# Routing by chunks with ScalarE normalising, and experts that gather their rows: one change to a two-layer graph and expert kernel on one core

## What is computed

```python
x = x + L0_gnn(layernorm(x), ...)
x = x + L0_ffn(layernorm(x))      # top 2 of 8 experts
x = x + L1_gnn(layernorm(x), ...)
x = x + L1_ffn(layernorm(x))      # top 1 of 8, with a capacity
# L0_ffn, on xt = layernorm(x):
probs = softmax(xt @ Wr + br)
top_p, top_idx = top_k(probs, 2); weights = top_p / top_p.sum(-1)
xn = layernorm(xt)                # normalised once more
xe = xn * ln_g[e] + ln_b[e]
y = gelu(xe @ W1[e] + b1[e]) @ W2[e] + b2[e]
out = sum of weights * y over the two experts chosen
# L1_ffn, on x = layernorm(x), C = ceil(1.25 * 6250 / 8):
idx = argmax(probs); pos = place of the token in its expert's list
y = (relu(x @ w1[e] + b1[e]) @ w2[e] + b2[e]) * probs[idx] * (pos < C)
y = nan_to_num(y, nan=0.0, posinf=10000.0, neginf=-10000.0)
```

## Time and profile before

| | us |
|---|---|
| median of 3 runs | 6620.97 (6618.58 to 6625.28) |
| profiled run | 6623.49 |
| its span in the trace | 6621.3 |
| plan, node and edge phases of layer 0 | 0 to 2479.2 |
| routing, layer 0 | 2479.2 to 2832.4 |
| experts, layer 0 | 2832.4 to 3662.2 |
| node and edge phases of layer 1 | 3662.2 to 5902.3 |
| routing, layer 1 | 5902.3 to 6163.3 |
| experts, layer 1 | 6163.3 to 6621.3 |

### The profile page before, as it was taken

The page is one execution under the profiler, slowest core; times in us unless marked ns, Lnnn a source line. Parts: engine busy times, 40 slices in busy tenths (PEclk is TensorE's granted clock), DMA queues, the critical chain, the costliest instruction groups (busy, mean ns, idle before and its releaser), DMA issues. The chain is left out here.

```text
span 6621.3 us, 95822 instructions
## 1 busy us (share of the span) xinstructions
PE 4812.8 (73%) x19729; PEld 3525.1 (53%) x19729; DVE 3271.2 (49%) x5938; ACT 1384.0 (21%) x2978; POOL 3635.1 (55%) x3707
## 2 busy tenths in 40 slices
PE   0699999999999982189999435655656565643798
PEld 0355555555555552179999424444444344433698
DVE  5666676666667657211111334444444453544244
ACT  1333333333333320022222201111111111101122
POOL 1677777777777730512222177777777777711322
PEclk9899999999999995589999768888888888875899
DMA  7565565655656626256666555555555555532455
GB/s 214 181 169 159 158 162 157 161 161 157 162 159 160 161 72 216 73 169 184 183 183 184 134 139 137 143 137 142 138 141 139 140 141 138 141 110 109 169 200 188
DMA packets 717638, 1021.21 MB, mean 154 GB/s; under 512 B 301763, under 2 KB 531271, under 8 KB 692316
## 3 DMA queue, kind: packets, MB, share of 16 engines
q0 software_dynamic: 183456, 485.95, 28.4%
q1 hardware_dynamic: 488760, 491.67, 24.8%
q10 hardware_dynamic: 45188, 41.42, 2.1%
HBM read 868.25 MB, written 152.93 MB: 154 GB/s over the span
## 5 line engine op out<-in xcount | busy, mean ns | idle before, releaser
L760 POOL DMA_INDIRECT e_rows<-sc_table,e_eidx x3224 | 3138.4, 973 | 1049.4 <-issue 956.3
L867 PE MATMUL e_ps_o<-e_rows,e_oh 128*128 128x264 f32 x6448 | 1655.6, 401 | 150.1 <-ACT e_res L953 134.3
L867 PEld LDWEIGHTS e_ps_o<-e_rows,e_oh 128*128 128x128 f32 x6448 | 1214.2, 196 | 588.5 <-issue 415.4
L1126 DVE TENSOR_TENSOR e_rows<-e_rows,e_ps_w 128x1024 f32<-128x1024 f32 x806 | 969.8, 1206 | 25.4 <-ACT e_rows L949 14.0
L1058 DVE SCALAR_TENSOR_TENSOR e_u<-e_encr,e_adst,e_ps_hd 128x512 f32<-128x512 f32 x806 | 593.2, 744 | 516.6 <-PE e_ps_X L809 414.0
L809 PE MATMUL e_ps_X<-e_u,e_hwide 128*104 128x512 f32 x1612 | 806.0, 593 | 0.0
L953 ACT COPY e_res<-e_ps_o 32x264 f32<-32x264 f32 x806 | 296.7, 368 | 2122.1 <-PE e_ps_o L871 1710.2
L1670 PE MATMUL x_ps_h<-x_xT,x_w 128*128 128x256 f32 x2624 | 647.8, 405 | 14.1 <-DMA x_b<-in_L_ffn_b_dram 14.1
L1670 PEld LDWEIGHTS x_ps_h<-x_xT,x_w 128*128 128x128 f32 x2624 | 638.3, 337 | 19.0 <-issue 14.9
L839 PE MATMUL e_ps_X<-e_ident,e_alog 128*104 128x128 f32 x496 | 100.3, 367 | 747.7 <-ACT e_alog L933 747.7
L1681 PE MATMUL x_ps_y<-x_w,x_hT 128*128 128x256 f32 x2624 | 579.9, 379 | 0.0
(11 more groups left out here) (290 smaller groups left out, 4067.1 us busy)
## 6 DMA issues: line engine op xcount, KB each, us to landing
x_w<-in_L_ffn_W_dram SPq DMA_DIRECT2D x112, 1024.0 KB
e_at<-sc_grp SPq DMA_DIRECT2D x403, 192.0 KB
x_w<-in_L_ffn_w_dram SPq DMA_DIRECT2D x60, 1024.0 KB
e_rows<-sc_table,e_eidx POOLq DMA_INDIRECT x3224
e_at<-sc_grp SPq DMA_DIRECT2D x403, 96.0 KB
sc_agg<-e_res ACTq DMA_DIRECT2D x806, 33.0 KB
sc_xb<-r_zero SPq DMA_DIRECT2D x24, 1032.0 KB
x_xin<-sc_xb SPq DMA_DIRECT2D x86, 258.0 KB
```

The costliest lines, as they stand in the source:

```text
L760: pool.indirect_dma_start(rows[:, k, s, j, :], None, dr["table"][:, :], bass.IndirectOffsetOnAxis(eidx[:, k, s, j:j + 1], 0)).then_inc(s_r ...
L867: nc.tensor.matmul(ps_o[:, 0:ROW], oh[:, k, at_j:at_j + P], rows[:, k, s, j, :], start=(j == 0), stop=False)
L1126: nc.vector.tensor_tensor(part, part, ps_w[:, k, :, s * HEADS:(s + 1) * HEADS].unsqueeze(3).to_broadcast([P, CH, HEADS, DH]), ALU.mult).th ...
```

## The change

**Routing.** The statistics are now finished chunk by chunk: `combine(c)` adds and takes statistics of chunk c, `finish(c-1)` turns the deviation that ACT made of the chunk before into a scale and an offset. ACT normalises each tile with these (L1411) and copies the turned tiles of two tiles before. PE turns `r_xt` directly, in three PSUM slots, and multiplies. In layer 0 the second normalising is folded into the scale, and the logits are multiplied by `r_std` in turn. SP saves the normalised rows once in token order, `xn0` (258 floats a row) or `xn1` (514, with the token's own row behind it), with each token's weights as 8 bytes behind its row. `xb`, its zeros and POOL's 98 and 49 scatters are gone. Slots become lists of tokens on PE: for each tile and choice DVE makes two matrices of zeros and ones, `r_ohl` [128 x 128] (place in a list) and `r_ohh` [128 x n_hi] (which list, times the token's number; n_hi is 120 in layer 0, 72 in layer 1), and PE sums `r_ohl`^T `r_ohh` over all tiles in `r_ps_t`: 98 products in layer 0, 49 in layer 1, through a ring of 14.

**Experts.** POOL gathers the rows of a block, two transfers a block, by `x_take`, a copy of a piece of the list. It gathers blocks 0 and 1 ahead of the loop; in the loop, for block n, it waits for s_add of block n, gathers block n+2, and then scatters block n. PE's `turn` waits for the gather (s_gx) where it waited for SP's load. SP loads weights only, w1 first. In layer 1 the token's row comes with the gather, so the separate gather of `x_xr` is gone. DVE no longer makes row numbers.

```diff
@@ routing, SP
-                for r0 in range(0, n_slot, 8 * P):
-                    n = min(8, (n_slot - r0) // P)
-                    sp.dma_start(xb[r0:r0 + n * P, :].rearrange("(p j) d -> p (j d)", p=P), zero[:, 0:n * XW]).then_inc(s_fill, 16)
+                    if c >= 2:
+                        keep_rows(c - 2)
+                    if c >= 4:
+                        even_rows(c - 4)
...
+                sp.wait_ge(s_wq, 1)
+                with nc.allow_non_contiguous_dma(reason="a token's weights behind its row, once"):
+                    sp.dma_start(xn[0:NP, D:XW].rearrange("(t p) d -> p t d", p=P), wgt[:, :, :]).then_inc(s_rows, 16)
@@ routing, POOL
-                for t in range(NT):
-                    pool.indirect_dma_start(xb[:, :], bass.IndirectOffsetOnAxis(slot_i[:, 0, t:t + 1], 0),
-                                            xt[:, t, :], None).then_inc(s_top[t // R], 16)
...
@@ routing, PE
+                for t in range(NT):
+                    turn(t)
+                    if t >= 2:
+                        logits(t - 2)
...
+                for n in range(top * NT):
+                    pe.wait_ge(s_ohl, n + 1)
+                    pe.wait_ge(s_ohh, n + 1)
+                    nc.tensor.matmul(ps_t[:, 0:n_hi], ohl[:, n % (2 * R), :], ohh[:, n % (2 * R), :],
+                                     start=(n == 0), stop=(n == top * NT - 1)).then_inc(s_inv, 1)
@@ routing, ACT
+                def even(c):
+                    act.wait_ge(s_nb, c + 1)
+                    for t in range(c * R, (c + 1) * R):
+                        nc.scalar.activation(xt[:, t, :], xs[:, t, :], ACT.Identity, bias=nb[:, t:t + 1], scale=rstd[:, t:t + 1]).then_inc(s_xtn, 1)
+                        if t >= 2:
+                            copy(t - 2)
...
@@ routing, DVE
+                for c in range(R):
+                    combine(c)
+                    if c >= 1:
+                        finish(c - 1)
+                finish(R - 1)
...
+                    for t in range(NT):
+                        n = c * NT + t
+                        if n >= 2 * R:
+                            v.wait_ge(s_inv, n - 2 * R + 1)
+                        nc.vector.tensor_scalar(ohh[:, n % (2 * R), :], iotah[:, :], hi[:, c, t:t + 1], mark[:, c, t:t + 1],
+                                                ALU.is_equal, ALU.mult).then_inc(s_ohh, 1)
+                        nc.vector.tensor_scalar(ohl[:, n % (2 * R), :], iotap[:, :], lo[:, c, t:t + 1], None, ALU.is_equal).then_inc(s_ohl, 1)
@@ experts, POOL
+                def gather(k):
+                    for s in range(SUB):
+                        pool.indirect_dma_start(xin[:, k, s, :], None, xn[:, :],
+                                                bass.IndirectOffsetOnAxis(take[:, k, s:s + 1], 0)).then_inc(s_gx[k], 16)
...
-                        hold(pool, s_ix, i * 8 + (4 * k + 4), s_pq)
-                        if not first:
-                            for s in range(SUB):
-                                pool.indirect_dma_start(xr[:, k, s, :], None, rows_in[:, :],
-                                                        bass.IndirectOffsetOnAxis(idx[:, k, s:s + 1], 0)).then_inc(s_gx[k], 16)
+                        hold(pool, s_ix, i * 2 + (k + 3), s_pq)
                         hold(pool, s_add, i * 2 + (k + 1), s_pq)
+                        gather(k)
+                        hold(pool, s_give, i * 2 + (k + 1), s_pq)
@@ experts, PE
-                        hold(pe, s_ldx[1 - k], (i + k) * n_ldx + n_ldx, s_pp)
+                        hold(pe, s_gx[1 - k], (i + k) * n_sc + n_sc, s_pp)
+                        if first:
+                            hold(pe, s_ldx[1 - k], (i + k) * n_ldx + n_ldx, s_pp)
                         turn(1 - k)
```

More of the change, by code:

```diff
@@ L1226, in ffn_phases @@
         cnt_i = keep("cnt_i", [1, 4], I32)
+        token = keep("token", [P, n_hi], I32)
+        choice = keep("choice", [P, n_hi, 2], F32)
         with ExitStack() as ctx:
@@ L1266, in ffn_phases @@
             ps_c = ps("ps_c", [P, 2, 512])
+            ps_t = ps("ps_t", [P, 512])
             s_x = [sem(f"x{c}") for c in range(R)]
             s_ag = [sem(f"ag{c}") for c in range(2)]
[L1269 to L1277, removed]
+            s_w, s_const, s_zero, s_chain, s_stat, s_var, s_std, s_nb, s_agu, s_xtn = (
+                sem(n) for n in ("w", "const", "zero", "chain", "stat", "var", "std", "nb", "agu", "xtn"))
+            s_t, s_xT, s_l, s_pick, s_cnt, s_soft, s_exp, s_wq, s_slot, s_ohl, s_ohh, s_inv, s_kept, s_rows = (
+                sem(n) for n in ("t", "xT", "l", "pick", "cnt", "soft", "exp", "wq", "slot", "ohl", "ohh", "inv", "kept", "rows"))
             block = ctx.enter_context(nc.Block())
@@ L1364, in logits @@
                     mm.then_inc(s_l, 1)
[L1366 to L1372, removed]
+                for t in range(NT):
+                    turn(t)
+                    if t >= 2:
+                        logits(t - 2)
+                logits(NT - 2)
+                logits(NT - 1)
@@ L1430, in _ @@
                         nc.vector.bn_stats(st[:, t, :], xs[:, t, :]).then_inc(s_stat, 1)
[L1432 to L1435, removed]
+                    v.wait_ge(s_stat, (c + 1) * R)
+                    m, d = mean[:, tiles], dif[:, :]
+                    tt(m, st[:, tiles, 1], st[:, tiles, 4], ALU.add)
                     ts(m, m, 0.5, None, ALU.mult)
-                    tt(d, st[:, :, 1], st[:, :, 4], ALU.subtract)
+                    tt(d, st[:, tiles, 1], st[:, tiles, 4], ALU.subtract)
@@ L1476, in red @@
                     done(nc.vector.tensor_reduce(o, i, AX_X, op))
+                ts(valid[:, :], iotan[:, :], float(N), None, ALU.is_lt)
+                v.wait_ge(s_l, NT)
+                if first:
+                    tt(lg[:, :, :], ps_l[:, 0:NT, :], wide(std[:, 1, :]), ALU.mult)
+                    tt(lg[:, :, :], lg[:, :, :], each(br[:, :]), ALU.add)
+                else:
+                    tt(lg[:, :, :], ps_l[:, 0:NT, :], each(br[:, :]), ALU.add)
                 red(c1[:, 0, :], lg[:, :, :], ALU.max)
@@ L1586, in ffn_phases @@
             s_gx = [sem(f"gx{k}") for k in range(2)]
-            s_ix, s_add, s_mul, s_fl, s_pq, s_free = (sem(n) for n in ("ix", "add", "mul", "fl", "pq", "free"))
+            s_ix, s_give, s_wc, s_wt, s_add, s_mul, s_fl, s_pq, s_free = (
+                sem(n) for n in ("ix", "give", "wc", "wt", "add", "mul", "fl", "pq", "free"))
             n_sc = 16 * SUB
-            n_ldx = 16 * (3 if first else 1)
+            n_ldx = 16 * 2
             n_ldw = 16 * 4
@@ L1646, in _ @@
                         pool.sem_inc(s_free, 1)
+                for k in range(2):
+                    hold(pool, s_gx[k], pairs * n_sc + n_sc, s_pq)
             @block.tensor
@@ L1728, in _ @@
                         affine(1 - k)
+                        hold(v, s_gx[k], i * n_sc + n_sc, s_pv)
+                        nc.vector.tensor_copy(take[:, k, :], token[:, bass.ds((i * 2 + (k + 2)) * SUB, SUB)]).then_inc(s_ix, 1)
+                        if first:
+                            nc.vector.tensor_tensor(wc[:, k, :, :], xin[:, k, :, D:XW], choice[:, bass.ds((i * 2 + k) * SUB, SUB), :],
+                                                    ALU.mult).then_inc(s_wc, 1)
+                            hold(v, s_wc, i * 2 + (k + 1), s_pv)
+                            nc.vector.tensor_reduce(wt[:, k, :], wc[:, k, :, :], AX_X, ALU.add).then_inc(s_wt, 1)
+                        hold(v, s_free, i * 2 + (k + 1), s_pv)
+                        nc.vector.tensor_copy(give[:, k, :], token[:, bass.ds((i * 2 + k) * SUB, SUB)]).then_inc(s_give, 1)
                         hold(v, s_y, i * 2 + (k + 1), s_pv)
-                        hold(v, s_free, i * 2 + (k + 1), s_pv)
                         for s in range(SUB):
```

283 lines of the change are left out of this document (151 added, 132 removed).

## The result

The changed kernel takes 6852.05 us in the median (6843.97 to 6857.54, 4 runs); the kernel before took 6620.36 beside it. The ratio is 1.0349 (95% interval 1.0336 to 1.0362): 3.5% slower. The forecast was slower, with 6645 and a range up to 6740; the direction held and the size did not, 207 us lie between. The profiled run took 6843.97, with a span of 6842.2.

The account below looks back on a forecast made before the run. It took DVE, then POOL's scatters, to bound layer 0's routing, and PE its experts. Routing -156 and -101, expert loops +104 and +127, clock +45, loop end +5 summed to +24: 6645 us, range 6520 to 6740.

Parts of the forecast that it names:

- A chunk: Routing, layer 0: a chunk of the statistics on DVE takes 12.2 us, where it took 10.51.
- A pair: Routing: two one-hot matrices on DVE and their product on PE, 0.46 us a pair, bounds 0.43 to 0.67.
- The 14 tiles behind the last chunk: Routing, layer 0: 14 tiles left for PE after the last chunk, 14 x 1.18 = 16.5 us, before the logits.
- Layer 1: Expert loop, layer 1: gather lands at 12.2 us, needed at 7.68; +4.7 a block, +127; low clock +45.
- Layer 0, landing: Expert loop, layer 0: gather waits behind weights, lands 9.5 us after h starts, 2.0 late a block: +104, ends 0 and 159.
- Layer 0, clock: Expert loop, layer 0: pauses of 2.0 us cost nothing through a lower PE clock (0 to 85).
- the second rival: Both expert loops: the clock falls after each pause, adding 53 x 1.6 us in layer 0: 6730; chance 0.12.
- The first rival: Expert loop, layer 0: gather lands before 7.68 us, so the 104 falls away: 6541, faster; chance 0.30.
- hidden parts: Routing, layer 0: row saving and 6272 weight pieces stay covered by other work; if not, 5 to 10 us.
- the loop's end: End of the expert loops: the last scatters stand behind two more gathers, 2 x 2.6 = +5 us.

Follow-up runs that it names:

- weights behind the issue: Changed kernel, but in layer 0 SP waits with a block's weights until POOL has issued both gathers: 6746.7 us.
- w1 in four: Changed kernel, but in layer 0 w1 is loaded as four transfers of 256 KB instead of one of 1 MB: 6739.5 us.

## Why the prediction was right in direction and wrong in size

**Routing: right in its sums, one step by luck.** -157 and -99 against -156 and -101. A chunk takes 11.9 (said 12.2); logits came 118.4 after the routing's start (said 116.1). A pair costs 0.45 to 0.46 (said 0.46), but on DVE (0.255 + 0.195): the forecast took its number from a row of PE and had DVE's pair between 0.33 and 0.48, so the match is luck. That PE's clock rose there to 0.84 and more (0.59 is the stage's mean) changed nothing, since DVE sets the pitch. The 14 tiles behind the last chunk were seen; that ACT's order, too, holds them was not.

**Layer 1: right.** The chain on DVE, POOL's issue and the landing made 12.66 us against 12.35 (12.2 and 0.15 from landing to turning), the gathers issued 0.6 sooner than said and the rest 0.9 longer; 4.8 of pause a block against 4.7; and the clock cost about 2.3 a block against 1.6.

**Layer 0, landing: the step that failed.** The sum took the landing at 9.5 us after the h phase's start; its upper end, 159 us, stands for 10.5. It was 11.7. The wait behind w1 was not the error: a landing at 9.5 has the first packet 2.2 before it, at 7.3, and it came at 7.1. What was mis-sized is the time behind that. The 2.3 us that a gather pair takes alone were kept for the time behind w1, and being served among w2's packets was counted as a gain (8 to 9). But there the gathers share the engines with w2 and the first scatter: in the block shown it took 4.0 us from their first packet to the end of their last, where it took 2.0 with no weights, and turning began 0.8 us later, where 0.15 was allowed. A pause of 3.75 in the mean instead of 2.0: +95. The trace of the kernel before held a sign of it. Right behind the five microseconds of the earlier trace rows, from 3065.7 to 3070.6, the scatters' 0.26 MB took nearly five more beside the weights:

```profile
q1 hardware_dynamic: 437, 1.18, 67.1%
q0 software_dynamic: 287, 0.26, 34.2%
```

**Layer 0, clock: the second.** "For layer 0's pauses of 2.0 I take nothing" failed with it: with 3.75 us the second rival's mechanism came in, at 1.8 a block: +96. Nothing was too little for 2.0 as well: in the two runs with shorter pauses (weights behind the issue, w1 in four) 17 of the 59 pauses between 1.9 and 2.6 us were followed by a slow y. No run held all its pauses at 2.0. The rivals were laid out as exclusive, each with its own price, but this one hung on the size that the forecast had least hold of. Longer pauses brought both terms at once, 95 + 96 of the 207 us; the range, built from one term at a time, ended at 6740.

**The first rival** had the gather's own time right and what the weights do to it wrong. With no weights in the queue the gather is in time (15.05). The rule that the engines go round between queues packet by packet (the Trainium skill, "DMA: Bandwidth & Descriptors", section "Queues, rings and completion order") was cited for it. It fits the five microseconds in which q0 and q1 are served side by side. Before them q1 alone was served, 2.6 us longer than a gather needs to its first packet with no weights (4.3 and 1.7). The page lets an engine drain a whole packet of several descriptors before it switches, and no run shows how many of w1's 8 KB pieces make one such packet; so that wait need not be against the rule, but reading it as one short piece, and the landing near 7.5 that came of it, was wrong.

**Other points.** POOL's list issues came 1.30 to 1.32 apart (priced at 1.29); hidden parts (saved rows, weights behind the rows) stayed hidden, in no chain of the routing; the loop's end, priced at +5, came 4 us sooner instead.

## What to carry to other kernels

A load that is turned from a plain transfer into a gather by list also moves to another engine's program, and what counts is which waits stand ahead of it there: put it behind the last read of its buffer, not behind the work on the result. Its latency is to be priced behind the megabyte that is queued just ahead of it and beside the one that follows, not alone. And where PE pauses in every turn of a loop, price the pause and the low clock behind it together: with the pauses of 3.3 to 4.9 us in the changed kernel they came as one.

## What the chip showed that was not expected

- A pair of gathers (0.26 MB) had its last packet 6.5 us after the h phase's start with no weights in the queue, 11.1 with w1 (1 MB) issued 0.8 us before it and w2 behind; q0 got no packet while w1 moved as one transfer, and got in after 0.57 MB when it came as four with smaller packets.
- Pauses of PE of 3.3 to 4.3 us a block held the mean clock at 0.91 and made y 8.3 in the mean instead of 7.07; pauses of 2.0 to 3.6 us did so behind some blocks and not behind others (25 of 53). 22 small turnings (2.57 us) in the pause were enough to bring y back behind 50 of loop 0's 53.
- A load of 1 KB (`x_lnb`) behind w1 in the same queue became the wait of PE, its last packet 0.5 us behind the gathers' last.
